# The experts' first product computed turned, with the weight tile as stationary operand and loaded per tile

## The reference

```
logits = xt @ gate_w.T ; scores = softmax(logits) ; top_vals, idx = top_k(scores, 2)
xs = xt[:, None, :] * weights[:, :, None]
for e in range(8):
    h  = silu(einsum('tkd,hd->tkh', xs, w1[e]) + b1[e])
    x2 = einsum('tkh,dh->tkd', h, w2[e]) + b2[e]
    x3 = einsum('tkd,hd->tkh', xs, w3[e]) + b3[e]
    y  = y + sum(x2 * x3 * mask, axis=1)
z = silu(xt @ sw1.T) * (xt @ sw2.T) @ sw3.T
out = x + gb * (y + z)
```

## Time and profile before

| | us |
|---|---|
| median of 3 runs | 2111.36 |
| lowest, highest | 2108.86, 2111.7 |
| profiled execution, its own time | 2111.3 |
| its span | 2109.6 |

### The profile page before, as it was taken

One profiled execution on the slowest core, in us unless ns is written; L12 is line 12 of the kernel. 1 busy time (PEld: TensorE's weight loads), 2 busy tenths in 40 slices (PEclk: granted clock), 3 DMA queues, 4 the chain that ended last, 5 costly groups with the idle time before them and its releaser, 6 DMA issues.

```text
span 2109.6 us, 24075 instructions
## 1 busy us (share of the span) xinstructions
PE 1836.4 (87%) x6340; PEld 774.3 (37%) x6340; DVE 1962.1 (93%) x1839; ACT 1525.2 (72%) x3152; POOL 1790.8 (85%) x607
## 2 busy tenths in 40 slices
PE   7899898989898888989898979788867599999997
PEld 3323332424232323333232424232312256555664
DVE  7989999999999999999999999999999977757776
ACT  5886879797988888776879797988877444434443
POOL 5679999999999999999999999999999633425544
PEclk9988898989898998989898989898977799999999
DMA  7746454453535363535445454536262583235554
GB/s 261 231 129 148 112 133 115 118 126 103 130 104 137 85 160 82 144 99 138 116 123 124 110 126 108 123 104 149 55 149 61 171 322 110 91 95 90 89 85 73
DMA packets 140070, 265.21 MB, mean 126 GB/s; under 512 B 21232, under 2 KB 43760, under 8 KB 138784
## 3 DMA queue, kind: packets, MB, share of 16 engines
q1 hardware_dynamic: 125344, 241.95, 42.9%
q0 software_dynamic: 13296, 17.80, 4.9%
q10 hardware_dynamic: 1296, 3.93, 0.5%
HBM read 194.40 MB, written 70.26 MB: 125 GB/s over the span
## 4 chain that ended last, share of the span: by engine, by line
PE 25%; ACT 24%; DVE 22%; issue 15%; POOL 11%; DMA 2%; SPq 1%; DVEq 0%; ACTq 0%; POOLq 0%
DVE hst L1645 15%; ACT psum L1280 9%; POOL hst L961 7%; PE psum L2334 6%; DVE dbu L1624 5%; PE psum L2249 5%; PE psum L2353 3%; ACT dbu L1312 3%; POOL dbu L949 3%; PE psum L2262 3%; PE psum L2091 2%; ACT L1209 1%; ACT sp_tmp L1249 1%; ACT dt L1244 1%; ACT sp_tmp L1246 1%
## 5 line engine op out<-in xcount | busy, mean ns | idle before, releaser
L961 POOL TENSOR_TENSOR hst<-hst,c_rep 128x2048 f32<-128x2048 f32 x254 | 1145.9, 4540 | 5.9 <-ACT state L1266 3.7
L1645 DVE TENSOR_TENSOR_SCAN hst<-psum,state,dbu 128x1024 f32<-128x1024 f32 x384 | 885.3, 2363 | 0.4 <-ACT psum L1280 0.4
L1280 ACT ACTIVATE psum<-dt_rep,neg_a 128x512 f32<-128x512 f32 (+1 forms) x1024 | 660.2, 676 | 151.3 <-DVE hst L1645 148.4
L1624 DVE TENSOR_TENSOR dbu<-psum,b_rep 128x2048 f32<-128x2048 f32 x176 | 403.2, 2291 | 5.0 <-PE psum L2076 5.0
L949 POOL TENSOR_TENSOR dbu<-dtu_rep,b_rep 128x2048 f32<-128x2048 f32 x80 | 364.1, 4551 | 14.8 <-DVE hst L1645 9.1
L2091 PE MATMUL psum<-hst,same 128*32 128x512 f32 x2048 | 276.2, 688 | 56.2 <-POOL hst L961 49.4
L2076 PE MATMUL psum<-dt,same 32*128 32x512 f32 x352 | 216.5, 697 | 115.2 <-DVE dbu L1624 106.4
L1645 DVE TENSOR_TENSOR_SCAN hst<-psum,dbu 128x1024 f32<-128x1024 f32 x128 | 286.9, 2284 | 10.5 <-ACT psum L1280 9.8
L2023 PE MATMUL psum<-xp,taps 128*128 128x512 f32 x512 | 239.0, 610 | 7.7 <-ACT sp_tmp L1246 6.3
L1070 POOL DMA_INDIRECT out_x<-h,target_u x71 | 110.9, 1562 | 131.1 <-DVE h L1941 52.4
L2091 PEld LDWEIGHTS psum<-hst,same 128*32 128x32 f32 x2048 | 66.8, 124 | 273.2 <-issue 166.8
(11 more groups left out here) (194 smaller groups left out, 2480.4 us busy)
## 6 DMA issues: line engine op xcount, KB each, us to landing
dt_rep<-dt_scratch SPq DMA_DIRECT2D x256, 256.0 KB, 4.8
dtu_rep<-dtu_scratch SPq DMA_DIRECT2D x320, 64.0 KB, 1.9
taps<-taps_scratch SPq DMA_DIRECT2D x64, 256.0 KB, 4.7
b_rep<-bc_scratch SPq DMA_DIRECT2D x64, 256.0 KB, 5.0
c_rep<-bc_scratch SPq DMA_DIRECT2D x64, 256.0 KB, 7.8
dt_scratch<-dt SPq DMA_DIRECT2D x48, 256.0 KB, 6.1
h<-slot_scratch SPq DMA_DIRECT2D x71, 129.5 KB, 2.1
sp_tmp<-t_scratch SPq DMA_DIRECT2D x16, 512.0 KB, 6.8
```

What stands on the lines that cost most here:

```text
L961: nc.gpsimd.tensor_tensor(h, h, c_rep[q % 2][:], ALU.mult).then_inc(prod_done, 1)
L1280: nc.scalar.activation(psum[:, PS_A + i, kept], dt_rep[:, G % 2, j, kept], ACT.Exp, scale=neg_a[:, q % 2, u, i:i + 1]).then_inc(exp_done, 1)
L1624: nc.vector.tensor_tensor(dbu[:, U % DBU, :, :], psum[:, PS_U:PS_U + 1, :].broadcast_to((P, NG, TB)), b_rep[U // UNITS % 2][:], ALU.mult). ...
L1645: nc.vector.tensor_tensor_scan(both(hst[:, U % RING, groups, :]), both(psum[:, PS_A + 2 * pair:PS_A + 2 * pair + 2, :]), both(dbu[:, U % D ...
```

## The change

The w1 part is computed turned. Its stationary operand is now the weight matrix, in four blocks of 128 x 128, and its moving operand is the turned tile (128 columns): `hidden_gate` makes the w1 part with hidden units on partitions, four products in bank 4 + s % 2. The w3 part stays as it was, on 256 columns (`hidden_linear`). Since the w1 part now comes out turned, `turn_hidden` and `copy_hidden` are gone: ACT's `silu_tile` reads PSUM in two halves of 128 x 128, adds the bias b1 (one number per partition, from a small table `b1`) inside the activation, and writes `hsT`. DVE's `bias_hidden` adds b3 to 256 columns only. The table of biases that SP loads is 1 MB instead of 2 MB.

The stationary operand does not come from the resident `w13`, whose first half still lies there: SP loads the 256 KB of the tile's expert from DRAM for every tile, in pieces of 1 KB, into `w1`, one of 2 buffers (`load_weights`). Tiles 0 and 1 are loaded ahead of the loop. The load for tile s + 2 is issued when PE is through with `hidden_gate(s)` (`h1_full`), and in SP's program it stands behind `load_tile(s + 4)`. SP and ACT also read the experts' numbers, 8 tiles at a time.

```diff
+            w13_rows = A["w13"].rearrange("p (a n) -> p a n", a=NE * KD)
+            def load_weights(s):
+                if s % IDS == 0:
+                    expert_of.update(enumerate(ids_of(mybir.EngineType.SP, expert_u, s, NE - 1), s))
+                sp.dma_start(w1[:, s % 2], w13_rows[:, bass.ds(expert_of[s] * KD, KD), 0:DM]).then_inc(w1_loaded[s % 2], 16)
...
+            for s in range(2):
+                load_weights(s)
...
             for s in range(TILES - 4):
                 sp.wait_ge(target_kept, s + 1)
                 sp.wait_ge(gate_done, s + 1)
                 wait_apart(sp)
                 load_tile(s + 4)
+                sp.wait_ge(h1_full, s + 1)
+                load_weights(s + 2)
+            for s in range(TILES - 4, TILES - 2):
+                sp.wait_ge(h1_full, s + 1)
+                load_weights(s + 2)
...
             def silu_tile(s):
-                act.wait_ge(hx_done, s + 1)
+                act.wait_ge(h1_full, s + 1)
                 if s >= 2:
-                    act.wait_ge(hs_turned, s - 1)
-                nc.scalar.activation(hs[:, s % 2, :], hx[:, s % 4, 0:DM], ACT.Silu).then_inc(hs_done, 1)
+                    act.wait_ge(y_full, s - 1)
+                for m in range(KD):
+                    nc.scalar.activation(hsT[:, s % 2, m * P:(m + 1) * P], psum[:, 4 + s % 2, m * P:(m + 1) * P], ACT.Silu,
+                                         bias=b1[:, bass.ds(expert_of[s] * KD + m, 1)]).then_inc(hsT_done, 1)
...
             for s in range(TILES):
-                if s > 0:
-                    copy_hidden(s - 1)
+                silu_tile(s)
                 if s + 1 < TILES:
                     copy_tile(s + 1)
-                silu_tile(s)
                 if s + 1 < TILES:
                     begin_gate(s + 1)
-            copy_hidden(TILES - 1)
...
-                nc.vector.tensor_tensor(hx[:, s % 4:s % 4 + 1, :], psum[:, 2 + s % 2:3 + s % 2, :],
-                                        b13[:, bass.ds(expert_of[s], 1), :], ALU.add).then_inc(hx_done, 1)
+                nc.vector.tensor_tensor(hx[:, s % 4:s % 4 + 1, :], psum[:, 2 + s % 2:3 + s % 2, 0:DM],
+                                        b3[:, bass.ds(expert_of[s], 1), :], ALU.add).then_inc(hx_done, 1)
...
+            def hidden_gate(s):
                 pe.wait_ge(xtT_copied, s + 1)
+                pe.wait_ge(w1_loaded[s % 2], 16 * (s // 2 + 1))
+                if s >= 2:
+                    pe.wait_ge(hsT_done, KD * (s - 1))
+                for m in range(KD):
+                    for k in range(KD):
+                        ins = nc.tensor.matmul(psum[:, 4 + s % 2, m * P:(m + 1) * P], w1[:, s % 2, k, m * P:(m + 1) * P],
+                                               xtT[:, s % 2, k * P:(k + 1) * P],
+                                               start=(m == 0 and k == 0), stop=(m == KD - 1 and k == KD - 1))
+                ins.then_inc(h1_full, 1)
...
-                hidden(s)
-                if s > 0:
-                    turn_hidden(s - 1)
+                hidden_gate(s)
+                hidden_linear(s)
                 if s + 1 < TILES:
                     turn_tile(s + 1)
-                if s >= 2:
-                    result(s - 2)
+                if s > 0:
+                    result(s - 1)
```

More of the change, by code:

```diff
@@ L368, in mixer_and_experts @@
         part = lambda at, n, m: flat[:, at * DM:(at + n * m) * DM].rearrange("p (n d) -> p n d", n=n)
-        hx = part(0, 4, 2)
+        hx = part(0, 4, 1)
         yt = part(8, 4, 1)
         xtT = part(12, 2, 1)
-        hs = part(14, 2, 1)
         hsT = part(16, 2, 1)
@@ L375, in mixer_and_experts @@
         row_gate = part(24, 2, 1)
-        b13 = sb3("b13", [P, NE, 2 * DM])
+        b3 = sb3("b3", [P, NE, DM])
+        b1 = sb3("b1", [P, NE * KD])
+        w1 = sb3("w1", [P, 2, KD, DM])
         ffn.close()
@@ L491, in mixer_and_experts @@
         xtT_copied = sem("xtT_copied")
+        w1_loaded = [sem("w1_loaded0"), sem("w1_loaded1")]
+        h1_full = sem("h1_full")
+        hsT_done = sem("hsT_done")
         hx_full = sem("hx_full")
         hx_done = sem("hx_done")
-        hs_done = sem("hs_done")
-        hs_turned = sem("hs_turned")
-        hsT_copied = sem("hsT_copied")
         y_full = sem("y_full")
@@ L816, in _ @@
             sp.wait_ge(t_stored, 16 * STEPS)
-            for dst, name in ((w13, "w13"), (b13, "b13"), (w2, "w2")):
-                src = A[name].broadcast_to((P, A[name].shape[1])) if name == "b13" else A[name]
+            sp.dma_start(b1[:], A["b1"]).then_inc(f_w_loaded, 16)
+            for dst, name in ((w13, "w13"), (b3, "b3"), (w2, "w2")):
+                src = A[name].broadcast_to((P, A[name].shape[1])) if name == "b3" else A[name]
                 sp.dma_start(dst[:].rearrange("p a b -> p (a b)"), src).then_inc(f_w_loaded, 16)
@@ L1542, in begin_gate @@
                                      ).then_inc(gate_begun, 1)
-            def copy_hidden(s):
-                act.wait_ge(hs_turned, s + 1)
-                if s >= 2:
-                    act.wait_ge(y_full, s - 1)
-                nc.scalar.activation(hsT[:, s % 2, :], psum[:, 4 + s % 2, 0:DM], ACT.Copy).then_inc(hsT_copied, 1)
+            act.wait_ge(a_tables, 2)
+            act.wait_ge(f_w_loaded, 16 * 5)
             for r in range(4):
@@ L1909, in _ @@
             dve.wait_ge(a_tables, 3)
-            dve.wait_ge(f_w_loaded, 16 * 4)
+            dve.wait_ge(f_w_loaded, 16 * 5)
             expert_of = {}
@@ L2314, in _ @@
             pe.wait_ge(a_tables, 3)
-            pe.wait_ge(f_w_loaded, 16 * 4)
+            pe.wait_ge(f_w_loaded, 16 * 5)
             pe.wait_ge(s_o_mul, 2 * NBLK)
@@ L2327, in turn_tile, with hidden_linear @@
                 ins.then_inc(xt_turned, 1)
-            def hidden(s):
+            def hidden_gate(s):
                 pe.wait_ge(xtT_copied, s + 1)
+                pe.wait_ge(w1_loaded[s % 2], 16 * (s // 2 + 1))
[7 more added lines that the diff above has]
+                ins.then_inc(h1_full, 1)
+            def hidden_linear(s):
                 if s >= 2:
@@ L2333, in hidden @@
                 for k in range(KD):
-                    ins = nc.tensor.matmul(psum[:, 2 + s % 2, :], xtT[:, s % 2, k * P:(k + 1) * P],
-                                           w13[:, bass.ds(expert_of[s] * KD + k, 1), :].rearrange("p a n -> p (a n)"),
+                    ins = nc.tensor.matmul(psum[:, 2 + s % 2, 0:DM], xtT[:, s % 2, k * P:(k + 1) * P],
+                                           w13[:, bass.ds(expert_of[s] * KD + k, 1), DM:2 * DM
+                                               ].rearrange("p a n -> p (a n)"),
                                            start=(k == 0), stop=(k == KD - 1))
                 ins.then_inc(hx_full, 1)
[L2339 to L2346, removed]
             def result(s):
-                pe.wait_ge(hsT_copied, s + 1)
+                pe.wait_ge(hsT_done, KD * (s + 1))
                 if s >= 2:
@@ L2414, in lay_out @@
     out["w2"] = w["2"].reshape(P, -1)
-    out["b13"] = np.concatenate([a["ffn_b1"], a["ffn_b3"]], axis=1).reshape(1, -1)
+    out["b1"] = a["ffn_b1"].reshape(NE, KD, P).transpose(2, 0, 1).reshape(P, NE * KD)
+    out["b3"] = a["ffn_b3"].reshape(1, -1)
     out["b2"] = a["ffn_b2"].reshape(1, -1)
```

11 lines of the change are left out of this document (6 added, 5 removed).

## The result

| | before | changed |
|---|---|---|
| median us | 2111.43 (4 runs) | 2185.85 (4 runs) |
| lowest to highest | 2108.86 to 2111.7 | 2183.84 to 2189.33 |
| span of the profiled execution | 2109.6 | 2182.1 |

The ratio is 1.0359 (95% interval 1.0345 to 1.0373): 3.6% slower. The forecast was 2177, with a range of 2145 to 2222. Of all executions behind this document one lies far outside (2670.84 us, of the kernel in which ACT copies the weights, with a mean granted clock of 0.64 where the others have 0.92), and it is left out of that kernel's ratio.

A forecast was written before the change was run, and what follows sets the result against it. PE bound the loop at 3.05 us per tile; the new ring through DVE, SP and the transfer would make it 4.03. 70 steps give +68.6 us, the shorter end -3: 2177 us, range 2145 to 2222.

The forecast's parts named there:

- PE's own work: PE in the expert loop: 2.84 us per tile after the change, 0.21 less, worth 15 us if PE stayed the bound.
- that rival: Longer 128-column passes in hidden_gate: +0.87 us in the ring, +0.43 per tile, 2207 us; 8%.
- The ring: hidden_gate(s), DVE on tile s, SP, transfer, hidden_gate(s + 2): 7.78 us for two tiles, 4.03 per tile with table reads.
- table reads: SP's two table reads in 8 tiles ahead of a weight load: 0.55 us each, 0.14 per tile.
- first product to DVE's start: Ring step from PE's first product of a tile to DVE starting on it: 2.06 us.
- transfer: Ring step from the weights' issue to landing: 2.85 us, from 2.1 for a tile load, 0.46 for packets, 0.3 for scatters.
- landing to PE: Ring step from the weights' landing to PE's start: 0.2 us.
- The DVE term: Ring step from DVE's start on the tile to the end of the instruction raising gate_done: 1.91 us.
- The clock rival: PE idling lowers its granted clock in the loop: about 4.7 us per tile, 2223 us; 10%.
- the transfer stays hidden: Rival: the weight load hides and PE's saving shows, 2096 us; 5%, another 2% for a draw.
- POOL allowing: Condition on the 2096 us: POOL's scatters keep pace, two taking 4.8 us, 2.4 a tile.
- The end: From the last hidden_gate to the end of the span: 13.2 us instead of 16.2, -3 us.

The follow-up runs named there:

- eight result buffers: The kernel in which ACT copies the weights from the resident matrix, with 8 result buffers instead of 4: 2099.3 us, ratio 0.9947 to the kernel before.
- no scatters: The kernel that loads weights ahead of the tile on SP, without POOL's scatters and the waits for them: 2086.86 us, ratio 0.989 to the kernel before.
- weights first: The changed kernel with SP loading tile s + 2's weights before it waits for gate_done and loads tile s + 4: 2122.13 us, ratio 1.0055 to before.
- four buffers: The changed kernel with four weight buffers instead of two, tile s + 4's weights loaded where s + 2's were: 2126.27 us, ratio 1.0077 to before.
- gate first: The changed kernel with DVE running gate_rows(s), which raises gate_done, before bias_result(s - 2): 2158.01 us, ratio 1.0222 to before.

## Why the prediction was right

**The bound moved as said.** PE's own work fell to 2.84 us a tile: the last two steps of the changed kernel, and nearly every step of the two kernels in which PE waits for neither weights nor scatters (eight result buffers, no scatters), show it. Passes of 128 columns with a full weight block cost 0.11 (eight in 1.05 us, the last one's end included); that rival is out. So is the ratio that the prediction had formed from the Trainium skill's "TensorE: Matmul & The Clock Gate", section "Back-to-back issue gap": it would have made `hidden_gate` 0.4 us longer.

**The ring** is shown by three kernels that open or shorten it without touching a byte of traffic: weights first (-64 us), four buffers (-60), gate first (-28). Its terms are set below against the turn above and against a mean. The mean is over the 34 turns of the even tiles (0 to 2, 2 to 4 and so on, 283.6 us in all), which set the pace: both table reads fall on them, and in 33 of the 34 PE starts 0.09 us behind the landing of the weights, while in 14 of the 33 odd turns the weights had landed earlier and PE was not free.

| us per turn of two tiles | forecast | the turn above | mean, even tiles |
|---|---|---|---|
| first product to DVE's start | 2.06 | 2.14 | 2.37 |
| DVE to the end of L1942 | 1.91 | 1.68 | 1.65 |
| `gate_done` to tile load | 0.22 | 0.21 | 0.22 |
| tile load to weights' issue | 0.54 | 0.53 | 0.53 |
| table reads | 0.28 | none | 0.32 |
| transfer | 2.85 | 2.77 | 3.15 |
| landing to PE | 0.2 | 0.09 | 0.11 |
| sum | 8.06 | 7.42 | 8.34 |

So the forecast's 4.03 us a tile stands against 4.17; over all 70 steps, the short first and last ones included, it is 4.13. The sum came within 0.28 us a turn because errors of both signs met, and that part is luck. DVE and the landing were too long by 0.35 us, 12 us in 70 steps; the transfer and the first product's way to DVE were too short by 0.61, 21 us. The net is nearly the 9 us between 2177 and 2186. In the transfer it is the tail that counts: the median of all loads was 3.0, but a ring pays the mean. In the first term 0.23 of the 0.31 us is the clock, see below.

The DVE term was misread. Rows 5 were taken for a pass in which DVE did not wait for PE's result, with 0.29 us from L1922 to L1937. But PE's `result` (L2353) ended only at 1907.43 there, and L1937 began 0.15 us behind it, too short a wait for a bracket. Where the result was ready, before the change too, L1937 began 0.06 us after L1922, as L1953 does after L1938 now:

```profile
1906.40 1.03 PE L2353 MATMUL psum<-w,h 128*128 x4
...
1929.18 0.14 DVE L1922 CAST target_u<-h 128x1 uint32<-128x1 f32 x1
1929.24 0.42 DVE L1937 TENSOR_TENSOR h<-psum,tin 128x256 f32<-128x256 f32 x1
```

**The clock rival** came true in small. PE idled about a quarter of the loop, and the granted clock was 0.96 over it, with seven short stretches at the lower level (1.2 GHz); before it was 1.00 throughout, and it is 1.00 again in the kernels that keep PE busy. The window from 1885 to 2165 us of the changed kernel:

```profile
1885.00:2165.00 280.00, 213.66 (x1211) 178.13 (x1210) 137.96 (x402) 94.29 (x268) 102.33 (x66) 0.96 0.58 126
```

One such step, behind 3.12 us of idle PE, whose eight passes took 2.05 us instead of 1.13:

```profile
1966.72 2.05 PE L2352 MATMUL psum<-h,w 128*128 128x128 f32 x8 [3.12 <-issue]
```

4% of 280 us is 11 us of full clock lost, of which PE could feel at most the share in which it was busy, 76%: 9 us at most. The ring shows 8 of them: on even tiles the way from the first product to DVE's start had a median of 2.14 us and a mean of 2.37, and 0.23 us in 34 turns are 8 us. The rival was 10% likely in my cases at a price of some 45 us over the forecast; its price is much smaller.

**Transfer.** The sum made from this kernel's rows (2.85) was nearer to the measured 3.0 than the fit of the Trainium skill's "DMA: Bandwidth & Descriptors", section "Anatomy of one DMA — SWDGE (gpsimd) path" (2.6 as an estimate, by a fit made for POOL's path). The scatters beside it are not what the fit lacks: with no scatter at all the loads took 2.9 us median.

**What I had not seen** is the traffic's own price. In the changed kernel it is covered by the ring: at 4.13 us a tile POOL keeps up well enough that no wait of DVE for a result buffer stands among its waits. In the prediction it stood only as the transfer's third of a microsecond. With the ring open it is some 20 us, and the rival "the transfer stays hidden" was priced at 2096 without it: hiding this transfer gives 2122, slower than before. The side of the forecast would have held even then. That rival's clause "POOL allowing" was the step to work out, and the chain of scatters is most of the reason: 4.6 us to land, and two in flight.

**Signs that did not hold.** The loss went the forecast way, but the changed profile was to show PE busy 70% (it is 76%), the clock at 1.00 (0.96), and POOL no longer waiting for its scatters: it waited 81.6 us for their landing, where it was 30.1 before.

**The end** was forecast at 13.2 us and is 15.3. The last tiles come 2.84 us apart, and POOL falls behind once more: the scatter of tile 68 starts at 2172.85, 2.7 us after DVE has it ready.

## What to carry to other kernels

A load that is issued behind another engine's release belongs to a ring, and its price is the ring's length divided by the number of buffers, less the bound's step; add up the ring from single rows, with the mean and not the median of what varies, and the time follows to a few tenths of a microsecond per step. Look in each row for a wait too short to be marked. Opening the ring may take no more than a change of order: put the load ahead of the wait that it does not need, which here gave back 64 of 75 us. And when a transfer is hidden, ask what else shares the DMA engines: here it was mostly the scatters that paid, and it is their landing that holds POOL up, not their issue: back to back they are issued 1.86 us apart, against a step of 2.84, and land 3.8 to 4.6 us after it.

## What the runs showed of the hardware

- The scatters' landing depends on the traffic beside them: 3.9 us median with 9.5 MB on SP's queue in a loop of 220 us, 4.1 with 27.5 MB in 305 us (the changed kernel), 4.5 with 27.5 MB in 241 us, with the same scatters.
- It goes the other way too: 256 KB of weights in pieces of 1 KB landed in 2.9 us median with no scatters beside them, in 3.5 with them, in the same program otherwise (weights first).
- Where its input was ready, DVE began the addition behind the small copy 0.06 us after the copy's start, before the change and after; where it waited for PE's result, 0.15 us behind that result's end.
